# A four-layer graph network on one core: the first norm's last rows in two pieces, and gathers of the two edge layers without a clear ahead of each

## The reference, cut to what matters

```
x = layernorm(x + layer0(x, edge weights, edge vectors, src, dst))   # messages from x[src], summed by dst
x = layernorm(x + layer1(x, src, dst))                               # three hops of a normalised sum, averaged
x = layernorm(x + layer2(x, src, dst, edge attributes))              # MLP on [x[src], x[dst], attr], max by dst
x = layernorm(x + layer3(x, src, dst, r_feat))                       # attention with two heads, softmax by dst
```

## Time and profile before

| what | value |
|---|---|
| median of 3 runs | 1765.17 us (1764.85 to 1766.4) |
| the profiled execution, own time | 1775.35 us |
| its span, first to last instruction | 1773.6 us |
| DVE busy | 1318.2 us (74%) |
| POOL busy | 1282.3 us (72%) |
| PE busy | 749.2 us (42%), granted clock 0.678 of full speed |
| ACT busy | 483.7 us (27%) |
| clears ahead of indirect DMAs (L764) | 830 |
| indirect DMAs of the edge layers (L774) | 88 for each |

### The profile page before, as it was taken

How to read it: one execution, slowest core, us unless ns; L and a number is a source line. 1 busy time by engine, 2 the same in 40 slices (tenths; PEclk the granted TensorE clock), 3 DMA queues, 4 the chain that set the end, 5 groups by cost and what they waited for, 6 DMA issues and landing times.

```text
span 1773.6 us, 14347 instructions
## 1 busy us (share of the span) xinstructions
PE 749.2 (42%) x3676; PEld 548.8 (31%) x3676; DVE 1318.2 (74%) x2358; ACT 483.7 (27%) x1063; POOL 1282.3 (72%) x1839
## 2 busy tenths in 40 slices
PE   7932545456415016406426000466406777652400
PEld 3311222222202015406326000465305667651400
DVE  9964789899989988774565997488766989986300
ACT  7913211111101024404324301334302344442100
POOL 8877788888788848857888378860078838888776
PEclk9965768688756558858668555778656766665655
DMA  8159311111110213303223430000001111110000
GB/s 325 52 157 363 106 24 27 27 32 33 26 18 14 65 70 100 117 27 123 81 70 126 158 112 6 6 25 21 30 13 24 36 26 36 30 30 10 10 11 10
DMA packets 61789, 114.23 MB, mean 64 GB/s; under 512 B 25309, under 2 KB 46344, under 8 KB 60920
## 3 DMA queue, kind: packets, MB, share of 16 engines
q1 hardware_dynamic: 24432, 80.96, 12.5%
q0 software_dynamic: 31296, 12.76, 5.0%
q10 hardware_dynamic: 5960, 19.43, 3.0%
HBM read 60.87 MB, written 55.21 MB: 65 GB/s over the span
## 4 chain that ended last, share of the span: by engine, by line
POOL 56%; DVE 18%; issue 18%; PE 4%; DMA 2%; ACT 1%; another core or an unknown queue 1%; POOLq 0%; ACTq 0%; SPq 0%; DVEq 0%
POOL A_dst L774 12%; POOL joined L774 12%; POOL out L917 11%; POOL A_msg L859 7%; POOL gtmp L764 6%; POOL work L774 3%; DVE work L1519 2%; DVE A_dst L1519 2%; POOL out_short L774 2%; POOL A_msg L774 2%; DVE work L2309 1%; DVE stat L1530 1%; DVE joined L1519 1%; DVE A_msg L2309 1%
## 5 line engine op out<-in xcount | busy, mean ns | idle before, releaser
L1343 PE MATMUL bank<-w2fold,work 128*128 128x384 f32 x392 | 198.0, 652 | 213.6 <-DVE work L1519 156.0
L764 POOL MEMSET gtmp<- 64x64 f32 x830 | 139.4, 168 | 191.6 <-DMA table<-A_dst 131.6
L1530 DVE TENSOR_REDUCE work<-work 128x80 f32<-128x1280 f32 (+3 forms) x147 | 205.6, 1432 | 79.4 <-ACT work L1051 51.0
L917 POOL DMA_INDIRECT out<-A_dst,out_i x196 | 216.8, 1106 | 59.9 <-POOL gtmp L764 33.1
L774 POOL DMA_INDIRECT A_dst<-in_x,dst_i x196 | 215.5, 1099 | 58.2 <-POOL gtmp L764 29.6
L774 POOL DMA_INDIRECT joined<-x_pos,A_tmp x168 | 174.5, 1039 | 48.9 <-POOL gtmp L764 37.8
L1343 PEld LDWEIGHTS bank<-w2fold,work 128*128 128x128 f32 x392 | 90.6, 250 | 319.2 <-issue 278.8
L1519 DVE TENSOR_TENSOR work<-bank,work 128x384 f32<-128x384 f32 (+1 forms) x294 | 154.7, 604 | 7.7 <-remote 4.6
L1383 PE MATMUL bank<-nodes_w,small 128*128 128x128 f32 (+1 forms) x784 | 124.0, 318 | 71.5 <-ACT small L1041 41.0
L1012 ACT ACTIVATE work<-A_tmp,b1col,w1col 65x256 f32<-65x256 f32 x98 | 58.8, 600 | 320.4 <-PE bank L1343 265.8
L774 POOL DMA_INDIRECT work<-table,pos_i x88 | 121.6, 1382 | 24.1 <-POOL gtmp L764 20.3
(11 more groups left out here) (394 smaller groups left out, 2167.8 us busy)
## 6 DMA issues: line engine op xcount, KB each, us to landing
work<-in_x SPq DMA_DIRECT2D x26, 960.0 KB
x_pos<-joined SPq DMA_DIRECT2D x13, 990.0 KB
out<-work ACTq DMA_DIRECT2D x13, 960.0 KB
A_tmp<-ew_turned_rows ACTq DMA_DIRECT2D x49, 130.0 KB
table<-A_dst SPq DMA_DIRECT2D x2, 3136.0 KB
edge_sums<-A_dst SPq DMA_DIRECT2D x2, 3136.0 KB
table<-A_dst SPq DMA_DIRECT2D x13, 448.0 KB
A_tmp<-in_edge_attr_2x SPq DMA_DIRECT2D x49, 112.0 KB
```

The source lines that it names most:

```text
L764: pool.memset(tile, 0.0).then_inc(cleared, 1)
L917: pool.indirect_dma_start(out=out, out_offset=bass.IndirectOffsetOnAxis(ap=out_i[:, t:t + 1], axis=0), in_=A_dst[:, t, :], in_offset=None, ...
L1343: last = nc.tensor.matmul(banks[2 * (u % PAIRS_DEEP) + j][:, 0:PATHS], hid_rows[:, u % PAIRS_DEEP, j * P:(j + 1) * P], w2_rows[:], start=T ...
L1530: return v.tensor_reduce(out=o, in_=a, axis=AX, op=op)
```

## The change

Two things. The first norm goes through eight pieces in place of seven chunks: the last chunk, columns 168 to 195, becomes a piece of 20 columns and one of 8. The last 8 destination columns raise a semaphore of their own, table 0 is stored in eight pieces, and ACT's and DVE's norm steps take the new order. And in the two edge layers the gathers of the first windows have no clear ahead of them: windows 3 and 0 of table 3 (16 + 24 = 40 columns), window 0 of table 4 (24 columns). The other windows keep theirs.

```diff
+UNCLEARED = (2, 1)
...
-TABLE_PARTS = [CHUNKS, 1, 1, CHUNKS, CHUNKS + 1]
+TABLE_PARTS = [CHUNKS + 1, 1, 1, CHUNKS, CHUNKS + 1]
...
-        dst_rows = [sem(f"dst_rows_{c}") for c in range(CHUNKS)]
+        dst_rows = [sem(f"dst_rows_{c}") for c in range(CHUNKS + 1)]
...
+        FIRST_PIECES = [*range(CHUNKS - 1), slice((CHUNKS - 1) * GATHER_CHUNK, T - ENDS), slice(T - ENDS, T)]
+
...
-            exchange(0, tmp_wide)
+            exchange(0, tmp_wide, FIRST_PIECES)
...
-                gather(lambda t: A_dst[:, t, :], x, dst_i, node_limit, lambda t: dst_rows[t // GATHER_CHUNK], columns,
+                gather(lambda t: A_dst[:, t, :], x, dst_i, node_limit, lambda t: dst_rows[t // GATHER_CHUNK + (t >= T - ENDS)], columns,
...
-                           range(first, first + slots), cleared_tile=gtmp[0:HF])
+                           range(first, first + slots), cleared_tile=None if i < UNCLEARED[k - 3] else gtmp[0:HF])
...
-            square, take_root = norm_steps(A_dst, scale=ONE_VAR / FEAT, bias=one_eps)
-            for c in range(CHUNKS):
-                square(c)
-                if c:
-                    take_root(c - 1)
-            take_root(CHUNKS - 1)
+            square, take_root = norm_steps(A_dst, order=FIRST_PIECES, scale=ONE_VAR / FEAT, bias=one_eps)
+            for i in range(len(FIRST_PIECES)):
+                square(i)
+                if i:
+                    take_root(i - 1)
+            take_root(len(FIRST_PIECES) - 1)
...
             def add_layer0(c):
-                v.wait_ge(dst_rows[c], 16 * GATHER_CHUNK)
+                k = c if isinstance(c, int) else FIRST_PIECES.index(c)
+                v.wait_ge(dst_rows[k], 16 * chunk(A_dst, c).shape[1])
                 return tt(chunk(A_dst, c), chunk(A_dst, c), chunk(A_sum, c), ALU.add)
 
-            norm(A_dst, add_layer0, first_table)
+            in_turn(*norm_steps(A_dst, add_layer0, first_table, order=FIRST_PIECES), parts=len(FIRST_PIECES))
```

## The result

The changed kernel takes 1752.15 us (median of 6 runs, 1749.03 to 1755.22), the kernel before beside it 1764.69 (6 runs, 1763.47 to 1766.4). The ratio is 0.9929, interval 0.9916 to 0.9942: 12.5 us faster (10.2 to 14.8). The forecast was 1752.1, and 13.1 us.

The account below looks back on a forecast made before the run. The prediction took POOL's successive indirect DMAs to set the end where the change acts. Its terms, 5.6 (layer2) + 3.3 (layer3) + 4.2 (norm) = 13.1 us, taken from 1765.17, gave 1752.1 us, range 1747.5 to 1758.5.

Parts of the forecast that it names:

- What bounds the kernel: Where the change acts, POOL's indirect DMAs, one behind another, set the end; POOL carries 56% of the chain, DVE 18%.
- Layer2's 40 clears, 5.6 us: Layer2's first windows: 40 clears gone at 0.14 us each gain 5.6 us, bounds 4.1 and 6.7.
- I take 5.6, the free pace: Layer2: value chosen between bounds 4.1 and 6.7, pricing all 40 columns at the 0.14 us seen without DVE work.
- the DVE moves that slow them shift by the same amount: Layer2: window 1's 24 cleared gathers and DVE's moves shift together, so window 0's gain is passed on.
- Layer3's 24 clears, 3.3 us: Layer3's window 0: 24 x 0.14 = 3.4 us, less one column, gives 3.3; other cases 2.3 and 4.0.
- The norm, 4.2 us: First norm's last chunk as 20 + 8: 3.9 us from DVE's tail plus 0.3 from the smaller store; bounds 3.0 and 4.8.
- DVE waited for POOL at the end of that stretch, so it costs nothing: After the first norm: POOL's 60 gathers begin 4.2 us earlier, DVE's node work only about 3, without loss.
- The sum: Whole kernel: 5.6 + 3.3 + 4.2 = 13.1 us faster, 0.74%, giving 1752.1 us.
- Rival A: DVE paces the gathers; only 30 columns beside idle or lightly working DVE gain, 4.2 us; with norm 8.4, 1756.8 us; chance 0.19.
- Rival B: The norm's split gives nothing, eaten by pushed gathers and the node work's new phase; 8.9 us left, 1756.3; chance 0.08.
- Rival C: The 64 uncleared gathers fall into DVE's rhythm at 1.66 us: 9.9 us slower, 1775.1; decides from mean 1.51; chance 0.03.

Follow-up runs that it names:

- the doubled clears: The changed kernel with two clears ahead of each of the 64 uncleared columns in place of none: 1777.31 us.
- the second profile of before: The kernel before profiled once more, nothing edited: own time 1763.86 us, span 1762.1.
- the clears alone: The kernel before with both edge layers' first-window clears (40 and 24) left out, the norm as before: 1754.65 us, ratio 0.9934.
- the kernel without clears: The changed kernel without any clear ahead of an indirect DMA (766 fewer): 1691.99 us; the kernel before without any clear takes 1690.96.

## Why the prediction was right, point by point

- **What bounds the kernel: right.** POOL's DMAs set the end; for the two edge layers the doubled clears show it from the other side, 24.6 us in the gathers and 25.2 in the time.
- **Layer2's 40 clears, 5.6 us: right in size, by two errors.** The gathers gain 6.8, about DVE's idle time, because "I take 5.6, the free pace" undervalued the columns under the scans. That "the DVE moves that slow them shift by the same amount" failed: 1.3 to 1.9 us come back there. Measured 6.0.
- **Layer3's 24 clears, 3.3 us: too low, and its upper bound of 4.0 too.** The gathers gain 4.5 in the traces; the measured 5.5 (3.2 to 7.6) is less sharp and leaves room for both. The mis-sized term is the 0.14 us for columns under the scans: the 1.39 us that the text itself derived from three scans was 1.37, so 0.24 each. The first gather, counted at nothing, gave 0.1 to 0.35 of it too (5.18 us to the next one in the second profile of before, 5.08 with layer3 alone uncleared, 4.83 with both layers uncleared).
- **The norm, 4.2 us: right where it acts, though by two errors, and wrong at the end.** Center of 640 elements 0.81 (0.82), tail 8.26 (8.3), POOL 58.09 - 53.79 = 4.30 us earlier relative to the norm's first addition (4.2). But the last rows were pushed more than the 1.0 us of the sum: their gather is issued 1.0 us later and they land 3.21 us after it in place of 2.52, 1.7 in all. And from the norm's end to the hop it is 2.20 us in place of 3.18, where the sum had 0.3 for the smaller store. The two errors cancel. The failed step is "DVE waited for POOL at the end of that stretch, so it costs nothing". DVE's lateness costs nothing there; but POOL's queue now meets DVE's long instructions and ACT's store at other places, and 2.2 to 2.6 us are lost, of which 1.8 are pinned to two places. That leaves 1.6 to 2.0 us. Measured 2.5 (0.9 to 4.1).
- **The sum** of 13.1 us came out at 12.5 because the norm's shortfall (4.2 to 2.5) and layer3's surplus (3.3 to 5.5) cancel. That 1752.1 meets 1752.15 is luck, the more so as the kernel before came out 0.5 us lower beside it; the range was not luck.
- **Rival A** is refuted by the clears alone, 11.7 us (9.2 to 13.9) where it had 4.2, by the pace of 1.37 under the scans and by the doubled clears. The row against it was the right one: a stall does not take back the columns gained before it. Its rule was half right. The Trainium skill, "SBUF — State Buffer", section "SBUF: two separate sides", says that of a DVE instruction with two inputs in SBUF and a GpSimd instruction that reads SBUF, the one that starts first keeps the shared port pair for its whole length and the other blocks. The gathers of 1032.94 and 753.84 agree, blocked until DVE was done. The pair at 1031.59 does not: DVE's instruction began at 1032.16, inside that gather, and took the 6.69 us that it takes elsewhere, and the gather took 1.05.
- **Rival B** (0.08) was part of the truth in this kernel (2.5 us of the 4.2 came out) and the whole of it without clears.
- **Rival C** is refuted: of the 64 uncleared columns none keeps a pace of 1.66 us; 1.37 is the slowest steady one. Its test, a mean of 1.51 us per column, was badly set, as it left out the blocked gathers: layer2's 40 columns have a mean of 1.72 us without clears, and still of 1.90 with them.
- **What it missed** is not in the sum: DVE's second wait in layer3, which the one execution at hand did not show, and that clears elsewhere hold 60 us more.

## What to carry to other kernels

A small instruction ahead of every DMA of a queue that sets the end is paid each time; price it separately for a free neighbour engine and for a busy one, as a blocked DMA ends on the neighbour's edges and can snap to the next earlier one. A head start given to an engine whose DMAs are blocked by another engine's long instructions, or held up behind another queue's large transfer, is worth only what the new phase leaves: here 4.2 us became 2.5, and 1.4 us of delay were gone at the end of the hop. A share of the chain, or the place where it leaves an engine, can differ as much between two profiles of one kernel as between before and after. Take a second profile before reading waits of a few us, when the first one's own time is off the median.

## What the runs showed of the hardware that I had not expected

- Gathers under back-to-back scans of 0.46 us keep in step with them: 1.37 us uncleared (three scans), 1.83 with two clears (four), and 1.61 with one, alternately 1.44 and 1.78 (seven for two).
- A gathered row whose DMA is issued while another queue moves a 960 KB store lands 3.53 us after its issue in place of 2.23. None of POOL's packets moved for 2.5 us, while the store alone held the 16 DMA engines at 99.3%.
- A second clear costs 0.20 us, with no second wait; a single one costs 0.14 though its row shows 0.17 us and a wait of 0.27, since without it 0.30 us of issue stand there.
- What the clears were put in for no run shows. Without them gathers do not fall to the 1.66 us of the earlier trace rows for good: the profile of the kernel without clears has the 196 destination gathers at 209.7 us busy and 59.7 idle, 1.37 each.
